# The shifted normed rows: one engine copies both halves out of PSUM instead of two engines one half each

## What is computed

```python
def shift_token(t):
    t1, t2 = jnp.split(t, 2, axis=-1)
    t2 = jnp.pad(t2, ((0, 0), (1, 0), (0, 0)))[:, :-1]
    return jnp.concatenate([t1, t2], axis=-1)
# in each layer:  h = shift_token(x);  q, k, v = split(h @ wqkv);  local attention;
#                 x = x + o @ wo;  h = layernorm(shift_token(x)) @ w1 + b1;  x = x + (a * gelu(g)) @ w2 + b2
x = x + 0.5 * _L0_ffn_ref(_layernorm(x), ...)     # two layers
x = x + _L0_attn_ref(_layernorm(x), ...)          # attention over the whole sequence
x = x + 0.5 * _L0_ffn_ref(_layernorm(x), ...)     # the two layers again
```

## Time and the profile before

| | us |
|---|---|
| three runs | 2654.19, 2656.12, 2656.79; median 2656.12 |
| the profiled execution | 2654.62, of which the span of the trace is 2652.7 |
| TensorE busy | 2553.2 (96% of the span) |
| VectorE busy | 2413.2 (91%) |
| ScalarE busy | 2336.3 (88%) |
| GpSimd busy | 2056.1 (78%) |

### The profile page before, as it was taken

One profiled execution on the slowest core, in us unless ns is written; L12 is line 12 of the kernel. 1 busy time (PEld: TensorE's weight loads), 2 busy tenths in 40 slices (PEclk: granted clock), 3 DMA queues, 4 the chain that ended last, 5 costly groups with the idle time before them and its releaser, 6 DMA issues.

```text
span 2652.7 us, 80662 instructions
## 1 busy us (share of the span) xinstructions
PE 2553.2 (96%) x29196; PEld 2088.5 (79%) x29196; DVE 2413.2 (91%) x6461; ACT 2336.3 (88%) x7364; POOL 2056.1 (78%) x2185
## 2 busy tenths in 40 slices
PE   6999999999999999998999899999999999999998
PEld 4787787877888888886998777787788788888876
DVE  7999999999999999995878999999999999999995
ACT  4899999999999999994444999999999999999995
POOL 7998889898888887881103989999898887788873
PEclk8999999999999999998999999999999999999999
DMA  3121111111111111110000111111111111111110
GB/s 100 44 53 28 28 40 28 32 28 35 28 30 30 28 42 28 30 32 4 8 1 8 31 28 30 28 41 28 28 28 35 30 34 32 38 39 36 36 40 25
DMA packets 63812, 83.96 MB, mean 32 GB/s; under 512 B 11538, under 2 KB 30652, under 8 KB 63420
## 3 DMA queue, kind: packets, MB, share of 16 engines
q1 hardware_dynamic: 63420, 78.82, 12.9%
HBM read 11.67 MB, written 4.19 MB: 6 GB/s over the span
## 4 chain that ended last, share of the span: by engine, by line
PE 65%; DVE 21%; ACT 7%; issue 4%; POOL 2%; DMA 0%; DVEq 0%; SPq 0%; ACTq 0%; POOLq 0%
PE PS L668 6%; PE PS L684 6%; PE PS L634 6%; PE PS L658 6%; PE PS L625 5%; PE PS L627 5%; PE PS L626 5%; PE PS L748 4%; ACT P L4780 3%; DVE SS L2294 3%; DVE T L2305 3%; DVE SQ L2313 3%; PE PS L729 3%; DVE MX L2348 2%; PE PS L650 2%
## 5 line engine op out<-in xcount | busy, mean ns | idle before, releaser
L4780 ACT ACTIVATE P<-PS,MX 128x128 f32<-128x128 f32 x2048 | 767.8, 463 | 2.1 <-DVE MX L2348 1.2
L6197 POOL TENSOR_TENSOR T<-T,SQ 128x512 f32<-128x512 f32 x512 | 654.0, 1283 | 68.1 <-DVE SQ L2313 54.4
L6233 POOL TENSOR_TENSOR P<-P,RI 128x512 f32<-128x512 f32 x512 | 526.7, 1040 | 113.3 <-DVE RI L2354 113.0
L4780 ACT ACTIVATION_READ_ACCUMULATOR P<-PS,MX 128x1 f32 x2048 | 568.0, 302 | 0.0
L6210 POOL TENSOR_TENSOR T<-T,RN 128x512 f32<-128x512 f32 x512 | 520.6, 1046 | 6.4 <-DVE RN L2342 6.1
L4787 ACT COPY PT<-PS 128x512 f32<-128x512 f32 x512 | 314.5, 697 | 77.3 <-PE PS L668 76.7
L4735 ACT ACTIVATE SQ<-PS 128x512 f32<-128x512 f32 x512 | 346.1, 678 | 34.9 <-PE PS L627 23.5
L2294 DVE TENSOR_REDUCE SS<-SQ 128x8 f32<-128x512 f32 x512 | 341.2, 675 | 25.9 <-ACT SQ L4735 22.4
L2305 DVE TENSOR_TENSOR T<-PS,TAB 128x512 f32<-128x512 f32 x512 | 349.6, 684 | 16.6 <-ACT SQ L4735 12.7
L625 PE MATMUL PS<-WH,YH 128*128 128x512 f32 x768 | 342.4, 446 | 10.3 <-POOL YL L6186 4.5
L2313 DVE TENSOR_TENSOR SQ<-PS,TAB 128x512 f32<-128x512 f32 x512 | 348.1, 680 | 3.4
(11 more groups left out here) (156 smaller groups left out, 6103.4 us busy)
## 6 DMA issues: line engine op xcount, KB each, us to landing
VP<-VP SPq DMA_DIRECT2D x480, 128.0 KB, 2.3
out_dram<-X SPq DMA_DIRECT2D x16, 256.0 KB, 2.6
X<-in_L_attn_x_dram SPq DMA_DIRECT2D x7, 512.0 KB, 4.5
SG<-in_L_ffn_w_dram SPq DMA_DIRECT2D x5, 341.0 KB, 3.3
SG<-in_L_ffn_wqkv_dram SPq DMA_DIRECT2D x4, 384.0 KB, 3.6
SGQ<-in_L_ffn_wqkv_dram SPq DMA_DIRECT2D x4, 256.0 KB, 3.6
X<-in_table_dram SPq DMA_DIRECT2D x2, 512.0 KB, 5.8
P<-in_L_ffn_wo_dram SPq DMA_DIRECT2D x2, 256.0 KB, 3.1
```

Source lines behind the costliest of these rows:

```text
L4780: ins = act.activation(P[:, g, p, :], PS[:, b, 128 * p:128 * p + 128], ACT.Exp, bias=MX[:, g, p:p + 1], accum_out=SM[:, g, p:p + 1])
L6197: pool.tensor_tensor(T1[:, k, :], T1[:, k, :], SQ[:, (2 * n + 1 - x) % 3, :], ALU.add).then_inc(added[x], 1)
L6233: pool.tensor_tensor(P[:, g], P[:, g], RI[:, g, :].unsqueeze(2).broadcast_to([128, NPAIR, 128]), ALU.mult).then_inc(p_scaled, 1)
```

## The change

ScalarE now makes both halves. `y0_down` copies partitions 64 to 127 first (one column further on), then partitions 0 to 63, and raises y0_low behind the second copy. In the first chunk of a sequence it writes the zero column itself, as a copy of an identity column with scale 0, ahead of its wait for the transposes. `y0_up` on VectorE is left only as the place of `add_b1` for t = 3 and 13; its other 62 calls are gone, and so is the semaphore y0_high, which the bank's next users and `split_y` waited for.

```diff
-               "LT": [y0_low, y0_high], "YT": [x_new], "NR": [normed]}
+               "LT": [y0_low], "YT": [x_new], "NR": [normed]}
...
-        def free_y0(t):
-
-            k = t % NCH // CPB
-            if t >= TURN and k < 2:
-                on.wait_ge(a_proj[V][1], NBATCH - 1 + k)
-                on.wait_ge(a_scored, 8 * (NBATCH - 1 + k))
-            elif t >= TURN:
-                on.wait_ge(a_valued, 8 * (NBATCH - 1 + k // 5))
-
         def y0_up(t):
-            if not exists("LT", t):
-                return
-            b, col = bank_of("LT", t), columns(t)
-            free_y0(t)
-            if first(t):
-                dve.memset(Y0[64:128, col:col + 1], 0.0)
-            on.wait_ge(ln_turned, outer(t))
             for l, when in B1_TURNS:
                 if t == when:
-                    add_b1(l, b)
-            dve.tensor_copy(Y0[64:128, col + 1:col + 1 + CH], PS[64:128, b, 0:CH]).then_inc(y0_high, 1)
+                    on.wait_ge(ln_turned, outer(t))
+                    add_b1(l, bank_of("LT", t))
...
         def local(phase):
...
                 rotate_sin(t - 3, 1, Q)
-                y0_up(t - 2)
                 rest_of_o(t - 5, 0)
...
                 y_next(s - 4)
-                y0_up(t - 1)
                 row_inverse(t - 4, 3)
...
             if layer(t) % 2 == 0:
                 on.wait_ge(y0_low, outer(t))
-                on.wait_ge(y0_high, outer(t))
...
         def y0_down(t):
             if not exists("LT", t):
                 return
-            col, k = columns(t), t % NCH // CPB
+            b, col, k = bank_of("LT", t), columns(t), t % NCH // CPB
...
+            if first(t):
+                on.wait_ge(const_in, 16)
+                act.activation(Y0[64:128, col:col + 1], ident[64:128, 0:1], ACT.Copy, scale=0.0)
             on.wait_ge(ln_turned, outer(t))
             for l, when in B1_TURNS:
                 if t == when:
                     on.wait_ge(b1_add, l + 1)
-            act.copy(Y0[0:64, col:col + CH], PS[0:64, bank_of("LT", t), 0:CH]).then_inc(y0_low, 1)
+            act.copy(Y0[64:128, col + 1:col + 1 + CH], PS[64:128, b, 0:CH])
+            act.copy(Y0[0:64, col:col + CH], PS[0:64, b, 0:CH]).then_inc(y0_low, 1)
```

More of the change, by code:

```diff
@@ L395, in build_program @@
     glu_done, y_new, x_new = sem("glu_done"), sem("y_new"), sem("x_new")
-    ln_stat, ln_mean, ln_var, ln_out, y0_high = [sem(n) for n in ("ln_stat", "ln_mean", "ln_var", "ln_out", "y0_high")]
+    ln_stat, ln_mean, ln_var, ln_out = [sem(n) for n in ("ln_stat", "ln_mean", "ln_var", "ln_out")]
     b1_add = sem("b1_add")
@@ L2517, in first_steps @@
             ln_stats(1)
-            y0_up(0)
             ln_aggregate(1)
@@ L2529, in first_steps @@
             rotate_sin(0, 1, K)
-            y0_up(1)
             sum_squares(0, 1, Q)
@@ L2572, in first_steps @@
             root(1, 4)
-            y0_up(2)
             root(1, 5)
@@ L2649, in first_steps @@
             root(3, 7)
-            y0_up(4)
             root(3, 8)
@@ L2721, in first_steps @@
             row_inverse(4, 0)
-            y0_up(6)
             rest_of_o(3, 0)
@@ L2753, in first_steps @@
             y_next(0)
-            y0_up(7)
             row_inverse(4, 3)
@@ L2806, in first_steps @@
             rotate_sin(7, 1, Q)
-            y0_up(8)
             rest_of_o(5, 0)
@@ L2839, in first_steps @@
             y_next(1)
-            y0_up(9)
             row_inverse(6, 3)
@@ L2892, in first_steps @@
             rotate_sin(9, 1, Q)
-            y0_up(10)
             rest_of_o(7, 0)
@@ L2925, in first_steps @@
             y_next(2)
-            y0_up(11)
             row_inverse(8, 3)
@@ L2978, in first_steps @@
             rotate_sin(11, 1, Q)
-            y0_up(12)
             rest_of_o(9, 0)
@@ L3064, in first_steps @@
             rotate_sin(13, 1, Q)
-            y0_up(14)
             rest_of_o(11, 0)
@@ L3097, in first_steps @@
             y_next(4)
-            y0_up(15)
             row_inverse(12, 3)
```

17 lines of the change are left out of this document (removed).

## The result

The changed kernel takes 2671.8 us (median of four runs, 2670.66 to 2672.13), the one before 2656.08 in the same session: 1.006 times as long, with an interval of 1.0042 to 1.0077. The forecast was 2651.5 in a range of 2641 to 2660. The direction was wrong, and the range too low by 12 us.

A forecast was written before the change was run, and what follows sets the result against it. It took TensorE as the bound, except first-layer stops at line 650 waiting for VectorE's `rotate_sin`. Its terms, -4.9 + 2.4 - 2 = -4.5 us on the median 2656.1, gave 2651.6, said as 2651.5 us, range 2641 to 2660.

The forecast's parts named there:

- the price on ScalarE: ScalarE's list: each of 64 added copies holds it 0.27 us from start to start, 0.54 us in a round.
- Term one: Line 650, odd chunk's second scores: without VectorE's copies, TensorE's stops shrink to 0.71 us each, -4.9 us in all.
- Term two: Line 729, even chunk: TensorE waits 0.2 us for ScalarE's lower copy where a sequence begins; +2.4 us, 0 to +5.
- Odd chunk: Line 650, first tile's scores: later lower copy delays TensorE 0.05 to 0.17 us, absorbed by the next stop; nothing taken.
- Ramps: Behind the attention, 1435 to 1580 us: ten VectorE copies go, -2 us (bounds 0 and 6.7); program start taken as 0.
- The one that ended slower: Lines 650 and 729: TensorE's bank hand-over behind two ScalarE copies becomes the bound; +6, 2662 us; chance 0.15.
- What would show it: Line 650's waits fall to about 0.7 us; new VectorE waits at `sum_squares` (0.3 to 0.5 us), `rest_of_o`; small line 729 waits.

The follow-up runs named there:

- no_shift: The changed kernel with one ScalarE copy of all 128 partitions at the same column, shift and zero column left out: 2653.95 us, 0.9993 of the kernel before.
- no_shift_low: `no_shift` with an extra ScalarE copy of 256 columns ahead of each, on partitions 0 to 63: 2656.9 us, 1.0005.
- zero_dve: The changed kernel with the zero column written by VectorE at its old place, under its own semaphore: 2665.27 us, 1.0037.
- sb_low: The kernel before, VectorE untouched, with 64 extra unread ScalarE copies that read and write partitions 0 to 63: 2657.61 us, 1.0008.
- sb_up: The kernel before, VectorE untouched, with 64 extra unread ScalarE copies that read and write partitions 64 to 127: 2667.81 us, 1.0048.
- no_shift_up: `no_shift` with an extra ScalarE copy of 256 columns ahead of each, on partitions 64 to 127: 2672.11 us, 1.0059.
- early: The kernel before, with most odd chunks' upper copy in ScalarE's idle time and TensorE's transposes of the rows moved ahead: 2655.87 us, 1.0002.
- o_first: The kernel before, with VectorE's even-chunk upper copy one place later, behind the first `rest_of_o`: 2655.68 us, 1.0001.
- q_first: The kernel before, with VectorE rotating the odd chunk's second queries 1.3 us earlier, ahead of the feed-forward statistics: 2694.42 us, 1.0146.
- odd_only: The changed kernel with only odd chunks' upper copies on ScalarE, even chunks' left on VectorE: 2659.0 us, 1.0015 of the kernel before.

## Why the prediction was wrong, point by point

- **"From start to start a copy holds it 0.27 us"** (the price on ScalarE): this is the step that failed. The 0.27 us in the earlier trace rows are the distance behind the *lower* copy. The upper one took 0.39 us to its successor and let 0.1 to 0.4 us of overlap with its predecessor go; together 0.51 us in the odd chunk and 0.81 in the even one. The trace of before had the warning in it. VectorE's upper copy is the one instruction of that shape, and it starts at 340.69, lasts 0.43 and is followed at 341.15: 0.03 us behind its end, no overlap. Three rows of VectorE from before show the pattern once more. L2430 works on partitions 0 to 63, L2432 and L2283 on 64 to 127:

```profile
353.48 0.73 DVE L2430 SCALAR_TENSOR_TENSOR Y<-PS,COLS,Y 64x512 f32<-64x512 f32 x1
354.22 0.76 DVE L2432 SCALAR_TENSOR_TENSOR Y<-PS,COLS,Y 64x512 f32<-64x512 f32 x1
354.90 0.43 DVE L2283 COPY Y<-PS 64x256 f32<-64x256 f32 x1
```

  Lower to upper: 354.21 to 354.22, no overlap. Upper to upper: 354.98 to 354.90, an overlap of 0.08 us. I had charged VectorE the 0.46 us from such rows and then priced the same copy on the other engine from a row of another kind. The length of the record, which the prediction weighed against the skill's figure, was not the matter: it is 0.37 us in either half.
- **The term's size**, by ratios of 2656 us: relief of VectorE -1.9, 64 more copies that overlap +3.2, their partitions +8.5, the column +6.1; sum +15.9 for 15.7 measured. (These are the steps from `no_shift` over `no_shift_low` and `zero_dve` to the changed kernel, so they must add up to the whole and prove nothing by it; each has an interval of 2 to 3 us either way. The 3.2 do not show in the rounds. The step of 8.5 for the partitions is 10 us between `sb_low` and `sb_up` and 14 between `no_shift_low` and `no_shift_up`.)
- **Term one, -4.9.** Half right. The stop at the second scores fell to 0.69 us where only VectorE was relieved, and even to 0.62 in the changed kernel; the squares do hold the sums (VectorE's wait at `sum_squares` is there, below). A shorter stop is no sign of relief, though: in `sb_up`, where VectorE's list is untouched, it fell to 0.65 us too (7.1 us in 11 stops), because TensorE comes to it later (0.26 us at the odd chunk's first scores, side by side with before). And the sum counted the whole of a shorter stop as won. By `no_shift` it was worth 1.9 us, ramps included, at the most 4.5: TensorE waits again further on, for ScalarE. The prediction looked for the next limit on the stopped step (what holds VectorE?) and not for the next stop behind it.
- **Term two, +2.4 (0 to 5).** Place, cause and order were right: line 729 waits for the lower copy, most where a sequence begins (+0.31, and +0.08 otherwise, 12 times each: 4.7 us, near the upper end of 5). The column was taken at 0.10 us; it holds ScalarE 0.21.
- **Odd chunk, 0.** The delay is 0.22 us and not 0.05 to 0.17, as the lower copy ends 0.26 us later than worked out (362.80; with the round's lateness of 6.37 us taken off, 356.43 for 356.17). It is indeed absorbed by the stop behind it, but it also takes from the stop what VectorE had won.
- **Ramps, -2.** Wrong in sign: until 115 us the changed kernel loses 3.4 us. Kernels that change nothing there (`early`, `o_first`, `q_first`) are 1.0 to 1.95 us late at that point too, so a good part is no effect of the change (last section). Behind the attention, from 1437 to 1565 us, where the 2 us were expected, the changed kernel becomes 0.95 us later, and `no_shift`, with VectorE relieved alone, gains 0.4.
- **Rivals.** The one that ended slower named the right engine and the right two places. Its mechanism, a hand-over of 0.3 us, is out: the lower copy ends at 362.80 and TensorE starts at 362.84, 0.05 us behind it before rounding.

```profile
362.84 0.41 PE L650 MATMUL PS<-MLOC,IDB 64*64 64x512 bf16 x4
```

- **What would show it.** The stops with two sizes gone (0.62 at the most of any), VectorE's new waits at `rest_of_o` and `sum_squares`, and line 729 all came, from 160 to 590 us (the one at `sum_squares` with 0.6 us a round for the 0.3 to 0.5 told):

```profile
DVE OTL L2344 <- ACT OTH L4745: 12.6, 23, 0.7
DVE SS L2278 <- ACT SQ L4686: 6.8, 29, 0.9
```

  This is the second lesson. Every sign that I had named for "right" was there, and the kernel was slower. All of them were waits. The sign that would have told was the length of a round.

## What to carry to other kernels

Price an instruction that moves to another engine by the distance from its predecessor's start to its successor's start, in a row with the same partitions on both sides, and look at the partitions from which its new neighbours read and write; its own record can be unchanged while its neighbours no longer run beside it. A stop that gets shorter is won only if the engines that the next waits depend on have time left in that stretch: look at their busy time there, not over the whole round. And check a forecast of a loop by the length of one round, since delays below the threshold of the list of waits add up to more than those in it.

## What the runs showed of the hardware

- **Partitions 64 to 127 on ScalarE.** A copy between neighbours that work from partition 0 starts only when the one ahead has ended if it reads or writes from partition 64 on (0.01 to 0.03 us behind it, where nothing else holds it); where all work from partition 0 it starts 0.1 to 0.4 us before that end. If it writes there, its successor waits as well (0.01 us behind it). If it reads SBUF there, the next instruction that reads SBUF from partition 0 waits too, even with four others between. The steps between two kernels with and without 64 such copies were 8.5, 10 and 14 us, 0.13 to 0.22 us a copy. The Trainium skill, page "ScalarE: Activation LUTs", section "What ACT_TABLE_LOAD costs", says that ACTIVATEs in a row overlap by about 93 ns; the traces agree for copies that start at partition 0 (0.10 us behind the lower copy, up to 0.37 where records are stretched) and show the exception. VectorE's rows above look alike, which was not tested by a run.
- **One element per partition** on those partitions held ScalarE 0.21 us, more than half of what 256 elements did (0.38).
- **ScalarE to TensorE** took 0.05 us from the lower copy's end to the matmul that takes over its bank, in 50 of the 64 cases of the changed kernel, for the 0.14 in the earlier trace rows.
- **The start has two forms.** At 47 us VectorE multiplies the tables of the second layer, four products from SBUF to SBUF, the shortest 0.68 us. Beside GpSimd's work they take longer, and not always as long. Before, then after the change (start, length of two products; the last row is the line's shortest, middle and longest record in ns):

```profile
47.38 2.15 DVE L2226 TENSOR_TENSOR TAB<-X 128x512 f32<-128x512 f32 x2
```

```profile
47.46 4.56 DVE L2226 TENSOR_TENSOR TAB<-X 128x512 f32<-128x512 f32 x2
...
48.43 3.04 POOL L6165 TENSOR_TENSOR T<-T,RN 128x512 f32<-128x512 f32 x3
```

```profile
L2226 DVE TENSOR_TENSOR TAB<-X x4: 677/1606/3952, 47.5 to 57.2; 128x512 f32<-128x512 f32 x4
```

  The profiled executions of before and of `odd_only` had the short form, all the others 4.5 to 5.5 us, `early` and `o_first` among them, which change nothing there and are 1.3 and 1.95 us late at 115 us. So 1 to 2 us between two profiled executions can be the start alone. The kernel before itself scattered from 2651.4 to 2657.8 us, but there is one trace of each kernel, so whether this is the reason is not shown. The Trainium skill, page "SBUF — State Buffer", section "SBUF: two separate sides", says that a VectorE operation with two SBUF inputs and a GpSimd operation that reads SBUF share a port that whichever starts first keeps for its whole instruction, while the other waits. The trace agrees in kind: the second product, 3.95 us long, ran from 48.07 to 52.02, and GpSimd's group of three ended at 51.47, 0.55 us before it, less than the 0.68 us that such a product takes alone. It differs in length, as the product was held over several GpSimd instructions and not one. No run here isolates it.
